# Twelve multiplications by the gates, moved on VectorE from P4's stage into Q2's stage

## The reference

```python
W = weights[condition]                          # one 64x64 matrix a sequence
y = jnp.einsum('bct,bcd->bdt', x, W)            # 4096 rows of 1024
scores = y @ Wr.T
top_vals, top_idx = jax.lax.top_k(scores, 16)
gates = jax.nn.softmax(top_vals, axis=-1)
G = jnp.zeros((N, K)).at[jnp.arange(N)[:, None], top_idx].set(gates)
h = jnp.einsum('nd,krd->nkr', y, A)
out = jnp.einsum('nkr,kdr->nd', h * G[:, :, None], B)
return x + 2.0 * out
```

## Time and profile before

| | us |
|---|---|
| median of three runs (707.06 to 707.44) | 707.3 |
| the profiled execution | 707.46 |
| its span, first to last instruction | 705.7 |
| TensorE busy in it | 700.4 (99%) |
| VectorE busy in it | 568.8 (81%) |
| ScalarE busy in it | 292.2 (41%) |

### The profile page before, as it was taken

The page is one execution under the profiler, slowest core; times in us unless marked ns, Lnnn a source line. Parts: engine busy times, 40 slices in busy tenths (PEclk is TensorE's granted clock), DMA queues, the critical chain, the costliest instruction groups (busy, mean ns, idle before and its releaser), DMA issues.

```text
span 705.7 us, 11098 instructions
## 1 busy us (share of the span) xinstructions
PE 700.4 (99%) x3822; PEld 608.5 (86%) x3822; DVE 568.8 (81%) x1022; ACT 292.2 (41%) x541; POOL 15.8 (2%) x22
## 2 busy tenths in 40 slices
PE   8999999999999999999999999999999999999998
PEld 8888888888888888988999888898899988888897
DVE  5888998897757899889795867987668496699885
ACT  5575554534535541444333542242334364233220
POOL 0000000100000000010000000001000000000100
PEclk9999999999999999999999999999999999999999
DMA  8976679787899998979989775868769987666886
GB/s 314 405 291 279 211 281 401 229 261 268 332 382 417 415 359 290 406 255 325 388 312 412 285 271 189 301 247 245 248 274 372 380 311 258 199 217 211 228 329 239
DMA packets 68937, 212.35 MB, mean 301 GB/s; under 512 B 10706, under 2 KB 13394, under 8 KB 68242
## 3 DMA queue, kind: packets, MB, share of 16 engines
q1 hardware_dynamic: 64802, 204.30, 78.0%
q0 software_dynamic: 2304, 4.20, 3.9%
q10 hardware_dynamic: 1776, 3.15, 1.2%
HBM read 150.80 MB, written 65.01 MB: 306 GB/s over the span
## 4 chain that ended last, share of the span: by engine, by line
PE 99%; DMA 1%; DVE 0%; issue 0%; DVEq 0%
PE Pb L755 40%; PE Pb L788 29%; PE Pb L809 13%; PE Cb L737 8%; PE S L852 4%; PE Pb L831 3%; DMA xc<-in_wts 1%; PE S L844 1%; PE T L907 0%; PE T L913 0%; PE Pb L771 0%; PE Cb L866 0%; PE S L866 0%; PE T L866 0%; DVE Q L1212 0%
## 5 line engine op out<-in xcount | busy, mean ns | idle before, releaser
L755 PE MATMUL Pb<-Op,Wt 128*128 128x512 f32 x888 | 214.2, 391 | 0.0
L755 PEld LDWEIGHTS Pb<-Op,Wt 128*128 128x128 f32 x888 | 165.4, 188 | 33.9
L788 PE MATMUL Pb<-Wt,Op 128*128 128x512 f32 x744 | 179.7, 391 | 0.0
L788 PEld LDWEIGHTS Pb<-Wt,Op 128*128 128x128 f32 x744 | 138.1, 188 | 28.1 <-DVE Op L1212 0.4
L1212 DVE TENSOR_TENSOR Q<-Pb,Q 128x512 f32<-128x512 f32 (+1 forms) x105 | 92.8, 901 | 27.9 <-issue 17.5
L1212 DVE TENSOR_TENSOR Op<-R,Op 128x512 fp32r<-128x512 f32 x100 | 66.6, 686 | 23.4 <-ACT Op L945 23.3
L755 PE MATMUL Pb<-Ox,Wt 128*128 128x512 f32 x300 | 75.3, 390 | 0.0
L998 ACT COPY R<-Cb 128x512 f32<-128x512 f32 x60 | 35.1, 587 | 91.2 <-PE Cb L737 91.2
L755 PEld LDWEIGHTS Pb<-Ox,Wt 128*128 128x128 f32 x300 | 56.0, 188 | 11.5
L945 ACT CAST Op<-R 128x512 fp32r<-128x512 f32 x100 | 58.3, 622 | 17.3 <-DVE R L1212 10.4
L1212 DVE TENSOR_TENSOR Cq<-Pb,Cq 128x1024 f32<-128x1024 f32 (+1 forms) x46 | 44.5, 966 | 24.3 <-issue 10.4
(11 more groups left out here) (118 smaller groups left out, 688.9 us busy)
## 6 DMA issues: line engine op xcount, KB each, us to landing
Wt<-Wd SPq DMA_DIRECT2D x201, 512.0 KB, 6.5
Wd<-Wt SPq DMA_DIRECT2D x56, 512.0 KB, 5.1
xc<-in_x SPq DMA_DIRECT2D x24, 512.0 KB, 5.4
Q<-in_x SPq DMA_DIRECT2D x16, 512.0 KB, 5.3
out<-Q SPq DMA_DIRECT2D x8, 1024.0 KB, 4.8
BR<-in_B SPq DMA_DIRECT2D x4, 1024.0 KB, 8.5
Q<-in_x SPq DMA_DIRECT2D x16, 256.0 KB, 5.6
out<-in_x SPq DMA_DIRECT2D x16, 256.0 KB, 5.9
```

What stands on the lines that cost most here:

```text
L755: t = e.matmul(Pb[:, j, :], Wt[:, k, a, 128 * c:128 * c + 128], part((USES1[m], s, c), z), start=fresh and (c, a, z) == (0, 0, 0), stop=(c ...
L788: t = e.matmul(Pb[:, i, :], part((USES2[m], s, c), a)[:, 128 * i:128 * i + 128], Wt[:, k, z, :], start=fresh and (c, a, z) == (0, 0, 0), s ...
```

## The change

In groups 2 to 4 the four multiplications of quarter q = 1 by the gates leave the loop over P4's four columns and are done in the loop over Q2's first four products, each right behind that of q = 0. In group 1 they stay where they are, in P3's stage.

```diff
                             for name, c in splits_first(s, m, j):
                                 lo(name, s, c)
                             gated(s, 3, j, 1)
-                            if s:
-                                gated(s, 1, j, 0)
                         if (m, j) in ((1, 2), (3, 2 if s else 3)):
                             top_a(2 * s + (m == 3))
...
                                 lo(name, s + (name == "y21"), k)
                             if m == 0 and c < 4:
                                 gated(s, 0, c, 0)
+                                gated(s, 1, c, 0)
                             elif m == 0 and c == 6:
                                 sum_s1(s, 0)
                                 e.wait_ge(v_s1, 4 * s + 1)
```

## The result

708.73 us (median of 19 runs, 708.34 to 709.39) against 707.34 before: 1.39 us slower, ratio 1.0019, 95% interval 1.0013 to 1.0026. The forecast was 708.8, made on the first three runs of before. The change is slower, and its interval lies on both sides of 0.2%, which is 1.41 us.

What follows compares the result with a forecast made beforehand. TensorE was taken as the bound, busy 700.4 of 705.7 us, with VectorE also at its limit in these stages. Terms 0 + 0 + 1.5 us gave 708.8 us for the median, 8 in 10 range 707.6 to 709.5.

Steps and rivals of the forecast that it cites:

- drain k = 4: Q2's stage, last group: VectorE's drain of product k = 4 starts at 637.25 against 635.39, 1.86 us late.
- first load of k = 6: Q2's stage, last group: this weight load waits for VectorE and starts at 637.99, against 636.52 in the present run.
- Taken out of P4's stage: P4's second drain can start 0.40 us earlier, but TensorE had not waited for it: gain 0.
- The load is 1.47 us late: Q2's stage, last group: product k = 6's weight load makes TensorE lose +1.5 us, between bounds of 1.42 and 1.54.
- The step of 0.602: VectorE's queue: successive operations start 0.602 us apart, used as each one's price; 13 such steps precede drain k = 4.
- Behind it: Q1's and Q6's stages, last group: VectorE runs 1.6 to 1.7 us late, slack 0.6, no second wait.
- Groups 2 and 3: Q2's stage there: extra work goes partly into VectorE's idle time; k = 6's load keeps slack 0.3, cost 0.
- A: Rival: no wait at k = 6, since late VectorE work may have unseen slack; 707.3 (+-0.3), chance 0.12.
- B: Rival: groups 2 and 3 wait at k = 6 too, 0.2 to 0.5 each, 709.3 to 709.8; chance 0.14 with D.
- C: Rival: faster, about 706.1, if P4's second drain had held Q2's product k = 3 in three groups; chance 0.04.
- D: Rival: a second wait in Q1's or Q6's stage of the last group, 709.3 and up; chance 0.14 with B.
- Chances: Whole kernel: faster by over 0.2% 0.04, within 0.2% 0.43, slower 0.53; one wait, 708.5 to 709.1, 0.70.

Runs made afterwards that it cites:

- two early: Kernel before, with columns 2 and 3 of q1 moved in group 4 only, done behind q0(0) and q0(1): 707.77 us against 707.18, ratio 1.0007.
- two: Kernel before, with columns 2 and 3 of q1 moved in group 4 only, done behind q0(2) and q0(3): 708.28 us against 707.54, ratio 1.0014.
- six: Kernel before, with the change in group 4 only and lo G11(0) and lo G11(1) computed twice there: 710.52 us against 707.51, ratio 1.0045.
- the late variant: Kernel before, group 4 only: all four multiplications leave P4's stage, three go behind drain k = 4: 707.87 us against 707.54, ratio 1.0005.
- the run with one operation more: Kernel before, with the change in groups 2 and 3 only and lo G11(1) computed twice there: 708.23 us against 707.51, ratio 1.0009.
- groups 2 and 3 alone: Kernel before, with the four multiplications moved in groups 2 and 3 only, group 4 as before: 707.38 us against 707.54, ratio 1.0000.

## Why the prediction was right

Its numbers, less the 0.52 of the shorter start-up, against the rows after:

| step | predicted | less 0.52 | after |
|---|---|---|---|
| P4's second drain starts | 628.28 | 627.76 | 627.74 |
| drain k = 1 | 631.22 | 630.70 | 630.69 |
| drain k = 4 | 637.25 | 636.73 | 636.70 |
| first load of k = 6 | 637.99 | 637.47 | 637.50 |
| Q1 starts | 639.7 | 639.2 | 639.20 |
| group 2: lo G11(1), drain k = 4 | 289.82, 291.64 | 289.30, 291.12 | 289.31, 291.12 |

- *Taken out of P4's stage: gain 0.* Right: 1.81 us of VectorE's time stood idle there afterwards, and nothing came of it.
- *The load is 1.47 us late, +1.5 from 1.42 to 1.54.* Measured 1.48 in the stages, 1.39 in the medians. The step of 0.602 carried it. Two small errors in it partly cancelled: the drain started 0.03 earlier than worked out and the load 0.11 after the drain's end, not 0.05. Of the prediction's two bounds for what a late load costs, its lateness less 0.05 or plus 0.07, the runs lie between: against when it was due (636.52 in before, moved with P7's start) the load was late by 1.50 here, 0.29 with two early, 0.78 with two and 2.70 with six, and TensorE lost 1.48, 0.28, 0.75 and 2.68. (The Trainium skill, "VectorE: DVE Perf Modes", section "The DRAIN you can't avoid", says that the next operation doesn't start until the pipe is empty; taken as the whole duration for each step, that is an estimate of some 2.6 us. The same section says that an operation that isn't held starts earlier, which the prediction left out, and this trace agrees with that: from 635.50 to 636.70 two operations of 0.69 have passed.)
- *Behind it: no second wait, backlog gone at the idle time by 654.68.* Right: lo S2(3) at 650.44, idle of 0.36 at 655.64. How near it was, the late variant showed: there lo S2(3) started 650.33 - 638.21 = 12.12 us behind Q1's start and TensorE lost 0.22, here 650.44 - 639.20 = 11.24. If the loss is about the lateness, as at k = 6, some 0.66 us was left, an estimate; the prediction had 0.6.
- *Groups 2 and 3: slack 0.3, cost 0.* The cost is right, by the run with them alone; the slack was 0.25, by the run with one operation more.
- *Rivals.* A falls with the wait, B with groups 2 and 3 alone, C with P4's earlier drain that gained nothing in any run, D with Q6's stage.
- *Chances.* The side of the 0.2% line was given as nearly even, 0.43 to 0.53, and 1.39 us lies 0.02 under it, as near as makes no difference; the interval doesn't place it.

## What to carry to other kernels

Work moved on an engine that isn't the bottleneck is priced by what stands behind it in that engine's queue: count the steps from the last point at which the engine must wait anyway to the operation that the bottleneck waits for, and compare with when it is wanted. Up to the slack it costs nothing, beyond it the whole step each; the engine's idle share over the span says nothing of this. Count from every such point (a floor) on the way: the one that gives the latest time decides, and use start-to-start spacing from the trace, not durations.

## What the runs showed of the hardware

The step of VectorE, 0.602 us at durations of 0.69, held to 0.01 over thirteen steps of three kinds of operation (from 628.88 to 636.70 in the last group). Between sum_s1 and sum_s2, where the code makes VectorE wait for the first, it was 0.72 (639.10 to 639.82).

Not expected: a wait for a weight transfer in Q5's stage of group 2, near 348 us, in nine of the ten experiments' profiles and in neither of the two main ones; the edits of the nine are of every kind above. Its load waits 0.19 to 0.75 us. One of them, in the run with two (load, then the chain's piece, start and length):

```profile
348.50 0.53 PEld L788 LDWEIGHTS Pb<-Wt,Op 128*128 128x128 f32 x3 [0.73 <-issue]
```

```profile
339.40 9.00 DMA Wt<-Wd
```

The transfer took 9.00 us. It is a slow one in every profile, before's too: there the transfer issued at the same place of the program (at 339.4) took 8.3 us from issue to landing, against a median of 6.5 for all blocks of weights. The twelve profiles line up by it:

| transfer, us | profiles | wait of the load, us |
|---|---|---|
| 7.6 to 8.3 | before, the change, groups 2 and 3 only | none |
| 8.5 to 8.6 | four | 0.19 to 0.32 |
| 8.8 to 9.0 | five | 0.56 to 0.75 |

So the block of weights lands with next to nothing to spare, and a few tenths of a microsecond in one transfer, which no edit touched, cost up to 0.64 us from P7 of group 2 to P7 of group 4 (346.25 with two early, 345.61 before). That this is part of the scatter that hides effects of 0.3 us in the medians is likely, but only the profiled executions show it; why the transfer is slow just there wasn't tried.
